# Four-bit feed-forward worked in pairs of token tiles with three-operand VectorE forms, and the rotary output projection issued one key tile later

## What is computed

```python
def fp4_quant_dequant(x):                 # blocks of 16 along the last dim
    xb = x.reshape(shape[:-1] + (shape[-1] // 16, 16))
    scale = jnp.maximum(jnp.max(jnp.abs(xb), axis=-1, keepdims=True) / 6.0, 1e-12)
    xn = xb / scale
    idx = jnp.searchsorted(_MID, jnp.abs(xn))
    return (_GRID[idx] * jnp.sign(xn) * scale).reshape(shape)
def _L0_ffn_ref(x, w_gate, w_up, w_down):  # 128 -> 352 -> 128
    gate = fp4_linear(x, w_gate)
    y = fp4_linear(x, w_up)
    h = jax.nn.silu(gate) * y
    return fp4_linear(h, w_down)
x = x + L0_attn_a(layernorm(x)); x = x + L0_ffn(layernorm(x))
x = x + L0_attn_b(layernorm(x)); x = x + L0_ffn(layernorm(x))
x = x + L1_attn_a(layernorm(x)); x = x + L1_ffn(layernorm(x))
x = x + L1_attn_b(layernorm(x)); x = x + L1_ffn(layernorm(x))   # L1_attn_b: 16 heads of 8, rotary, 2nd output projection
```

## Time and profile before

| | |
|---|---|
| median of 3 runs | 2182.06 us (2181.73 to 2183.76) |
| profiled execution, its own time | 2174.85 us |
| its span | 2173.1 us |
| busy: TensorE, VectorE, ScalarE, GpSimd | 85%, 78%, 62%, 48% |
| mean granted TensorE clock | 0.941 of full speed |
| the two `fh` stages | about 103 us each |
| the `rt` stage | about 250 us |

### The profile page before, as it was taken

One profiled execution on the slowest core, in us unless ns is written; L12 is line 12 of the kernel. 1 busy time (PEld: TensorE's weight loads), 2 busy tenths in 40 slices (PEclk: granted clock), 3 DMA queues, 4 the chain that ended last, 5 costly groups with the idle time before them and its releaser, 6 DMA issues. The chain is left out here.

```text
span 2173.1 us, 36764 instructions
## 1 busy us (share of the span) xinstructions
PE 1839.4 (85%) x12003; PEld 885.4 (41%) x12003; DVE 1694.3 (78%) x2431; ACT 1356.1 (62%) x2314; POOL 1044.8 (48%) x1121
## 2 busy tenths in 40 slices
PE   5558886687886857999999999999999867789997
PEld 2123332543574412555555555555554423222222
DVE  5979996596347967888888888888887646798884
ACT  3547773444333435777777777777776534688984
POOL 0167773363005614666666666666666621431112
PEclk9779998699997978999999999999999988999998
DMA  3000000000000011121221222121121100422210
GB/s 96 0 15 0 0 0 0 1 1 1 0 0 0 1 55 33 42 62 62 62 62 62 62 62 58 57 58 59 62 61 62 46 20 16 101 76 56 60 45 39
DMA packets 71434, 84.49 MB, mean 39 GB/s; under 512 B 20544, under 2 KB 44032, under 8 KB 71168
## 3 DMA queue, kind: packets, MB, share of 16 engines
q1 hardware_dynamic: 69536, 81.69, 12.9%
q10 hardware_dynamic: 1728, 0.67, 0.1%
HBM read 71.95 MB, written 9.57 MB: 38 GB/s over the span
## 5 line engine op out<-in xcount | busy, mean ns | idle before, releaser
L1745 DVE SCALAR_TENSOR_TENSOR fu_kv<-fu_ps_kv,fa_vec,fu_kv 128x511 f32<-128x511 f32 (+2 forms) x384 | 286.0, 745 | 58.0 <-ACT fu_kv L1617 52.8
L1828 POOL TENSOR_TENSOR fu_ds<-fu_p 128x768 f32<-128x768 f32 x64 | 115.9, 1811 | 183.7 <-PE fu_ps_ss L1516 183.4
L2183 ACT ACTIVATE rt_p<-rt_ps_s 128x1024 f32<-128x1024 f32 x192 | 183.3, 1029 | 25.5 <-PE rt_ps_s L2114 25.5
L1476 PE MATMUL fu_ps_s<-fu_qn,fu_kn 64*128 64x512 f32 (+3 forms) x1024 | 190.0, 468 | 1.2 <-ACT fu_p L1676 0.8
L625 POOL TENSOR_TENSOR scan_hC<-scan_h,scan_c 128x1024 f32<-128x1024 f32 x64 | 150.9, 2358 | 71.5 <-DVE scan_h L601 71.5
L1617 ACT ACTIVATE fu_kv<-fu_ps_kv,fa_vec 128x512 f32<-128x512 f32 x128 | 88.3, 690 | 109.4 <-PE fu_ps_kv L1525 66.9
L1506 PE MATMUL fu_ps_n<-fu_p,fu_vt 128*64 128x512 f32 (+3 forms) x1024 | 151.9, 439 | 0.0
L601 DVE TENSOR_TENSOR_SCAN scan_h<-scan_dA,scan_ps_b 128x1024 f32<-128x1024 f32 x64 | 146.4, 2287 | 2.2
L524 PE MATMUL scan_ps_y<-scan_hC,w_ident 128*128 128x512 f32 x256 | 125.5, 613 | 26.4 <-POOL scan_hC L625 14.8
L2079 POOL TENSOR_SCALAR rt_d<-rt_d 128x1024 f32<-128x1024 f32 x32 | 35.0, 1094 | 182.7 <-DVE rt_d L2204 177.0
L1844 POOL TENSOR_TENSOR fu_kn<-fu_ks,fu_rb 128x512 f32<-128x512 f32 x64 | 81.5, 1274 | 74.2 <-DMA fu_rb<-rms_rows 74.2
(11 more groups left out here) (384 smaller groups left out, 5277.3 us busy)
## 6 DMA issues: line engine op xcount, KB each, us to landing
fu_rb<-rms_rows SPq DMA_DIRECT2D x256, 128.0 KB, 2.9
fu_ro<-rms_rows SPq DMA_DIRECT2D x128, 128.0 KB, 3.0
ra_stackq<-rope_parts SPq DMA_DIRECT2D x168, 32.0 KB
ra_stackk<-rope_parts SPq DMA_DIRECT2D x168, 32.0 KB
w_X<-in_xT SPq DMA_DIRECT2D x4, 512.0 KB, 7.8
fa_wp<-in_wp SPq DMA_DIRECT2D x8, 256.0 KB
fa_cr<-ncum_rows SPq DMA_DIRECT2D x128, 3.0 KB
rope_parts<-ra_hi SPq DMA_DIRECT2D x16, 128.0 KB, 2.5
```

What stands on the lines that cost most here:

```text
L1476: pe.matmul(sps[:, h, at:at + T - t * P], k[head(h), t * P:(t + 1) * P], q[head(h), t * P:T], start=(at == 0), stop=False)
L1745: dve.scalar_tensor_tensor(acc, kvps[:, at, 0:T - j], vec[:, a % GA, w:w + 1], acc, ALU.mult, ALU.add).then_inc(done, 1)
L1828: pool.tensor_tensor(DS[:, :, :], P0[p % 2][:, :, P:T], P13[:, :, 0:3 * P], ALU.add).then_inc(s.d1, 1)
L2183: act.activation(p[:, :, :], sps[unit(g, t, i) % RING][:, :, :], ACT.Exp, scale=DH_B ** -0.5).then_inc(s.exp, 1)
```

## The change

The `fh` stage now handles two token tiles with one instruction wherever before it needed two. `gps` and `ups` become one PSUM buffer of two banks each; the PSUM banks so freed go to a second buffer for the turns (`tps`) and one for the down product (`yps`). The product is written to a new SBUF tile `h` (three buffers) and is 704 elements wide (2 x 352), as are the maxima, the scaling and the total. The scales, the scaling and the total use the form with a scalar and two tensors (SCALAR_TENSOR_TENSOR); for the scales the second tensor is a constant column read with step zero. The larger-of-two of `sizes` leaves VectorE: ScalarE now computes it as Relu(size - ROUND) + ROUND in two more instructions (`over`, `limited`). The order of all lists is rewritten. GpSimd's instructions are the same, but the first waits for the total of both tiles. In the `rt` stage `project` moves from key tile 0 to key tile 1, and VectorE's `residual` moves behind `second`.

```diff
-                for k, v in enumerate((LN_EPS, RMS_EPS, 1.0, 10.397207708399179)):
+                for k, v in enumerate((LN_EPS, RMS_EPS, 1.0, 10.397207708399179, -ROUND, ROUND, ABOVE * 1e-12)):
...
-            gps = [st.ps(f"g{k}", [P, FF]) for k in range(2)]
-            ups = [st.ps(f"u{k}", [P, FB, FQ]) for k in range(4)]
-            tps = st.ps("t", [P, KF, P])
-            yps = st.ps("y", [P, T])
+            gps = st.ps("g", [P, 2, T])
+            ups = st.ps("u", [P, 2, T])
+            tps = [st.ps(f"t{k}", [P, KF, P]) for k in range(2)]
+            yps = [st.ps(f"y{k}", [P, T]) for k in range(2)]
+            h = [st.sb(f"h{k}", [P, 2, FB, FQ]) for k in range(3)]
...
+                    for k in range(PAIRS + LAG + 1):
+                        if real(k + 1):
+                            ups_of(k + 1)
+                        if k > LAG and (k - LAG) % 2 == 0:
+                            down((k - LAG) // 2 - 1)
+                        if real(k - LAG):
+                            turn(2 * (k - LAG))
+                        if real(k + 2):
+                            gates(k + 2)
+                        if real(k - LAG):
+                            turn(2 * (k - LAG) + 1)
...
+                    def over(k):
+                        act.wait_ge(s.size, k + 1)
+                        act.wait_ge(s.q, max(2 * k - 2, 0))
+                        act.activation(mag[k % 2][:, :, :, :], size[k % 2][:, :, :, :], ACT.Relu, bias=w.below_round).then_inc(s.over, 1)
+                    def limited(k):
+                        act.wait_ge(s.over, k + 1)
+                        act.activation(mag[k % 2][:, :, :, :], mag[k % 2][:, :, :, :], ACT.Identity, bias=w.at_round).then_inc(s.mag, 1)
...
+                    def scaled(k):
+                        hk = h[k % 3][:, :, :, :].rearrange(blocks)
+                        dve.wait_ge(s.inv, k + 1)
+                        dve.scalar_tensor_tensor(hk, hk, 1.0, widen(inv[k % 4][:, :, :].rearrange("p e a -> p (e a)"), FQ), ALU.mult, ALU.mult).then_inc(s.xn, 1)
+                    def total(k):
+                        dve.wait_ge(s.mag, k + 1)
+                        dve.wait_ge(s.q, max(2 * k - 2, 0))
+                        dve.scalar_tensor_tensor(tot[k % 2][:, :, :, :], mag[k % 2][:, :, :, :], 1.0, h[k % 3][:, :, :, :], ALU.mult, ALU.add).then_inc(s.tot, 1)
+                    for k in range(PAIRS):
+                        product(k)
+                        maxima(k)
+                        scales(k)
+                        if k >= 5 and k % 2 == 1:
+                            residual((k - 5) // 2)
+                        scaled(k)
+                        if k:
+                            total(k - 1)
...
-                        if t == 0 and closed(g - 6):
+                        if t == 1 and closed(g - 6):
                             project((g - 6) // GROUPS)
...
                     if on:
                         shifted(g)
+                    if on:
+                        second(g)
                     if closed(g - 6):
                         residual((g - 6) // GROUPS)
                     if on:
-                        second(g)
                         fourth(g)
```

More of the change, by code:

```diff
@@ L891, in down @@
                         pe.wait_ge(s.ht, 2 * NT * (m + 1))
-                        pe.wait_ge(s.x, m)
+                        pe.wait_ge(s.x, max(m - 1, 0))
                         for c in range(KF):
-                            rows = min(P, FF - c * P)
-                            i = pe.matmul(yps[:, :], w.down[0:rows, c, :], HT[m % 2][0:rows, c, :], start=(c == 0), stop=(c == KF - 1))
+                            inner = min(P, FF - c * P)
+                            i = pe.matmul(yps[m % 2][:, :], w.down[0:inner, c, :], HT[m % 2][0:inner, c, :], start=(c == 0), stop=(c == KF - 1))
@@ L896, in down @@
                         i.then_inc(s.y, 1)
-                    for j in range(2):
-                        gate(j)
-                        up(j)
-                    for k in range(-1, G // 2 + LAG):
-                        for e in range(2):
-                            if real(2 * (k - LAG) + e):
-                                turn(2 * (k - LAG) + e)
-                            if k >= 0 and real(2 * k + 2 + e):
-                                up(2 * k + 2 + e)
-                        for e in range(2):
-                            if real(2 * k + 4 + e):
-                                gate(2 * k + 4 + e)
-                        if k > LAG and (k - LAG) % 2 == 1:
-                            down((k - LAG) // 2)
+                    gates(0)
@@ new lines, in _ @@
+                    ups_of(0)
+                    gates(1)
+                    for k in range(PAIRS + LAG + 1):
[9 more added lines that the diff above has]
+                            turn(2 * (k - LAG) + 1)
@@ L928, in turned @@
                         act.wait_ge(s.y, max(m - 1, 0))
[L929 to L936 removed]
+                        act.activation(HT[m % 2][:, 0:2, t * P:(t + 1) * P], tps[j % 2][:, 0:2, :], ACT.Copy).then_inc(s.ht, 1)
@@ new lines, in limited @@
+                    def limited(k):
+                        act.wait_ge(s.over, k + 1)
+                        act.activation(mag[k % 2][:, :, :, :], mag[k % 2][:, :, :, :], ACT.Identity, bias=w.at_round).then_inc(s.mag, 1)
+                    gated(0)
+                    for k in range(PAIRS + LAG):
+                        if real(k + 1):
+                            gated(k + 1)
+                        if real(k - LAG):
+                            turned(2 * (k - LAG))
+                        if real(k):
+                            sized(k)
+                            over(k)
+                        if real(k - LAG):
+                            turned(2 * (k - LAG) + 1)
+                        if real(k):
+                            limited(k)
@@ L967, in total @@
-                    def total(j):
-                        dve.wait_ge(s.mag, j // 2 + 1)
-                        dve.tensor_tensor(tot[j // 2 % 2][:, j % 2, :, :], mag[j // 2 % 2][:, j % 2, :, :], ups[j % 4][:, :, :], ALU.add).then_inc(s.tot, 1)
-                    for k in range(G // 2 + 1):
-                        both = (2 * k, 2 * k + 1) if k < G // 2 else ()
-                        for j in both:
-                            product(j)
-                        if k:
-                            sizes(k - 1)
-                            total(2 * k - 2)
-                            total(2 * k - 1)
-                        for j in both:
-                            maxima(j)
-                        if both:
-                            scales(k)
-                        for j in both:
-                            scaled(j)
-                        m = (k - 4) // 2
-                        if k >= 5 and k % 2 == 1:
-                            dve.wait_ge(s.y, m + 1)
-                            dve.tensor_tensor(X[:, m, :], X[:, m, :], yps[:, :], ALU.add).then_inc(s.x, 1)
@@ L993, in _ @@
+                    for k in range(PAIRS):
[5 more added lines that the diff above has]
+                        scaled(k)
+                        if k:
+                            total(k - 1)
+                    total(PAIRS - 1)
+                    for m in range((PAIRS - 5) // 2 + 1, B):
+                        residual(m)
                 @block.gpsimd
@@ L994, in _ @@
                 def _(pool):
-                    for j in range(G):
-                        pool.wait_ge(s.tot, j + 1)
+                    for j in range(2 * PAIRS):
+                        pool.wait_ge(s.tot, j // 2 + 1)
                         pool.wait_ge(s.hq, max(j - NT + 1, 0))
```

100 lines of the change are left out of this document (47 added, 53 removed).

## The result

The changed kernel takes 2161.02 us (median of 4 runs, 2157.18 to 2162.46) where the kernel before takes 2181.96 (4 runs beside it): ratio 0.9911, 95% interval 0.9888 to 0.9935, so 14 to 24 us less. Forecast were 2168 us, that is 14 less, and a range from 2160 to 2182, so the time lies inside the range by 1 us. The profiled execution took 2161.56 us with a span of 2159.8, against 2174.85 and 2173.1. So the two traces lie 13.3 us apart and the medians 21. That gap of nearly 8 us is one of the things to explain.

What follows compares the result with a forecast made beforehand. The prediction took VectorE to bound the fh stage, busy 55.55 of 57 us. Two fh stages at 8 us less each and 2 us more in the rotary part gave -14, so 2168 us, range 2160 to 2182.

Steps and rivals of the forecast that it cites:

- Prices and holds: VectorE's fh instructions: product 0.89 us, reduction 0.885, scales 0.19; two-SBUF-input forms wait for GpSimd, except their first 0.14 us.
- The order of grants: VectorE and GpSimd turns in one fh period: periods 4.92 us, 5.19 with residual addition; first to last scales 72.8.
- The premise: VectorE in fh: instructions with two SBUF inputs are held by GpSimd; wide ones with at most one are not.
- GpSimd wins the race: Rival, fh: GpSimd's third instruction precedes the scales; periods 5.18 and 5.47, stage 4 us less, 2176 us; chance 0.17.
- Half rate: Rival, fh: scaling and total run at half rate, 1.62 us each; 44 us more, 2212 us; chance 0.01.
- Not held: Rival, fh: new forms never wait for GpSimd; periods 4.15 us, then TensorE binds; 2158 to 2162 us; chance 0.08.
- reduction held: Rival, fh: the reduction also waits for GpSimd; periods 5.4 and 5.7 us, stage even, 2183 us; chance 0.09.
- ScalarE bound: Rival, fh: ScalarE's queue sets the pace; periods about 5.2 and 6.4 us, 2187 us; chance 0.12.
- the tail: End of fh, last scales to stage end: 15.4 us against 15.8, a second down buffer letting the down product start early.
- The head: Start of fh: the first product waits for both tiles of gate and up, costing some 0.4 us.
- the rotary part: Rotary stage: the moved projection delays a copy and value product by 0.3 us in seven slots; 2 us more, bounds 0 and 3.
- The sum: Whole kernel: 16 us less from both fh stages, 2 us more from rotary; 14 less, 2168 us.

Runs made afterwards that it cites:

- Light GpSimd: Changed kernel with GpSimd's two feed-forward operations cut to 32 of 352 columns, so it computes something else, for timing only; 2155.4 us, ratio 0.990 to the kernel before.
- reciprocals in PSUM: Changed kernel with the reciprocals moved to the second down product's PSUM bank, leaving one down buffer; 2153.09 us, ratio 0.989 to the kernel before.
- two-operand forms: Changed kernel with plain tensor_tensor for the scaling and the total, operands unmoved; 2163.55 us, ratio 0.994 to the kernel before.
- larger-of-two on VectorE: Changed kernel with the larger of size and ROUND back on VectorE instead of two ScalarE passes; 2173.57 us, ratio 0.998 to the kernel before.
- filled tail: Changed kernel with unread TensorE products added at the end of each fh stage; 2163.4 us, ratio 0.995 to the kernel before.
- feed-forward alone: Changed kernel with the two rotary edits taken back; 2165.93 us, ratio 0.993 to the kernel before.
- rotary alone: Kernel before with only the two rotary edits; 2178.25 us, ratio 0.999 to the kernel before.

## Why the prediction came out as it did

**Prices and holds: right.** Product 0.88 (forecast 0.89), reduction 0.89 (0.885), scales 0.20 (0.19), scaling and total 0.88 when not held (0.89). The order of grants worked out from the earlier trace rows gave both periods and the stretch within 0.1 us. Light GpSimd shows the cause; reciprocals in PSUM and two-operand forms show that for the scaling it hangs on the second SBUF input and not on whether the form has two operands or three. The premise was too narrow in one respect: the scales of the kernel before (186 to 585 ns) and the larger-of-two on VectorE (0.51 to 1.10 us) are TENSOR_SCALAR instructions with one input in SBUF, and are held as well. So one input doesn't free an instruction of every kind; the reduction, with one, was free. The Trainium skill, SBUF — State Buffer, section SBUF: two separate sides, states this as an exclusive lock between GpSimd and a VectorE instruction that has two SBUF inputs or uses a two-port mode, which whoever starts first keeps for a whole instruction; the traces agree, but for the 0.13 to 0.16 us of the waiting instruction that are already done. No run tells which mode the one-input cases used.

**GpSimd wins the race: wrong, narrowly.** The scales were ahead by 0.09 us in the period shown (0.07 in the working), and with 203 to 206 ns they were never held in either stage.

**Half rate: wrong.** The rule of the Trainium skill named in the prediction (Vector Engine (DVE) Microarchitecture Reference, section Points that are easy to get wrong) would by the prediction's estimate make scaling 1.62 us; unheld it takes 0.88.

**Not held, reduction held: wrong.** Total 1.455 at the median; reduction 0.885 to 0.887. (The held reduction was also added up a little high: periods of 5.4 and 5.7 give 79.2 for the stretch, 1.6 less than before, and so some 2181 and not 2183.)

**ScalarE bound: wrong for this kernel, but it was next.** Its busy time is 42.44 of 57 us, 3.8 for an average pair (4.1 forecast), passes 0.87 to 0.88. As soon as the hold is gone, its queue sets the odd period, at 5.55 and 5.79, by much the mechanism given there. The prediction has the copies between magnitude and `over`; by the kernel's list one tile's stand ahead of the magnitude and the other's between `over` and `limited`, and the wait of 2.08 us lies ahead of the magnitude.

**The step that failed first: the tail.** "With two buffers it starts early and ends before GpSimd's last result": it ends 0.8 us before it, but at the lower clock, with turns of earlier tiles queued behind it. The term was 0.4 less and measured 1.0 and 0.5 more (17.67 and 17.40 from the last scales to the table load, 16.67 and 16.93 before). So the stages gained 6.7 and 7.8 us, not 8.0. In the first, 16.8 us from the last scales to the end stand against 15.4 forecast: 0.4 is GpSimd held by the last total, 1.0 comes after its last result. Where a stage of this form had a shorter seventh down product (4.26 us, two-operand forms, first stage; 2.85, filled tail, second stage) its last scales lie 16.74 and 16.76 from the table load, so the clock is worth 0.6 to 0.9. The head came as forecast in the first stage, 0.4 more, and cost nothing in the second.

**The second: the rotary part had the wrong sign.** The slot was read rightly and oversized: 0.26 us late after the copy, of which 0.18 is left per sequence, and the last projection starts 1.3 us later in the stretch (243.6 after the first exponential, 242.3 before) where 2 was forecast. Missing was the end of the stage: with the old order the granted clock fell before the last projection (2.07 us in the trace of before, 2.08 in the feed-forward alone) and was still low in the next stage; with the new one it didn't (1.12 us; the stretch is the same in all nine traces with it). From the last projection on, that gives 3.5 back (24.0 us before, 20.5 after), 0.95 on the projection and 2.3 on the centring products among it: net -2.2, not +2.

**The sum.** By the stages it is -6.68 - 7.75 - 2.20 = -16.6, where -14 was forecast. The errors of tail and rotary part have opposite signs, so that the forecast comes this near is partly luck. The second, larger comparison of medians measures -16.6 too, but that agreement proves little, because stretches that the change doesn't touch differ between traces. From the end of the second `fh` stage to the first rotary exponential it is 1110.6 us before, 1113.0 in the changed kernel and 1116.4 in its repetition. In the two first traces the untouched stretches together took 3.3 more, hence 13.3; that the span came out at 2159.8, where 2159 was forecast, is luck as well. The 21 of the first medians has an interval of 14 to 24. What the prediction could not see in one trace is that the old `fh` stages can be 3.0 and 4.2 us longer, as they are in the trace of rotary alone.

**Open.** Why moving a projection by 1.5 us, long before the end, decides whether the clock falls in the idle end of the stage. TensorE's busy and idle times there read the same in both orders. The runs show only that it is the clock and that added products prevent it. How often the clock is low at the last down product of the old `fh` stage is known from two traces, one each way. And why the long untouched stretch takes 1112.6 to 1117.3 us in the eleven traces with the new feed-forward (larger-of-two on ScalarE), and 1108.5 to 1111.8 in the other three: whether that is chance or a cost of the change no run tells. It is also the least certain part of how the measured gain is made up.

## What to carry to other kernels

Where VectorE and GpSimd alternate, write down for each VectorE instruction how many of its inputs lie in SBUF, find in the trace whether its kind is ever held (TENSOR_SCALAR was, with one input), and play through one period by the order of starts; here that gave the pace to 0.1 us. One operand moved to PSUM took 0.5 us off the even period, until the next queue bound, so look at once for what would then wait: here a copy in front of ready work. Ask also what the parts of a change bring by themselves: here the move of one operation to the idle ScalarE was nearly all of the stretch's gain. At the end of every stage look at the granted clock: a down product of 2.84 or 5.4 us at an uncovered place is a term as large as the change's parts, and it differs between executions, so read it from more than one.

## What the runs showed of the hardware that was not expected

The granted clock fell while TensorE was still at work: busy 0.97 of 2 us at 1.00, then 1.16 of 3 at 0.67, with the longest idle time 1.20 us (filled tail). Without added products it fell at a fixed place in both traces with the old order of the rotary stage (266.3) and in none of the nine with the other (264.0 to 264.2), but at varying places in the same `fh` program. And the residual addition took 0.68 us with one PSUM buffer for the down product (0.67 with the reciprocals in PSUM), 0.63 with two; no run looked into that.
